# A two-layer GRU with a mixture of experts between its steps: in six groups of steps the experts' products stand behind layer 1's products of a slot instead of behind layer 0's

## The reference

```python
mixed = tanh(x @ W_in.T + b_in + context)
# a GRU layer, twice: h1 = gru(mixed), h2 = gru(h1)
xg = x @ Wih.T + bih                       # for all steps
def step(h, xt):                           # 1024 steps, one after the other
    hg = h @ Whh.T + bhh
    r = sigmoid(xr + hr); z = sigmoid(xz + hz)
    n = tanh(xn + r * hn)
    return (1 - z) * n + z * h
x = x + ((1 + sigmoid(context @ W_gate.T + b_gate)) * h2) @ W_out.T + b_out
# mixture, for every token: a shared expert (512 wide) and 2 of 8 experts (256 wide)
shared = silu(x @ w1) * (x @ w3) @ w2
routed = sum over the 8 experts of combine[e] * (gelu(x @ W1e[e]) @ W2e[e])
out = x + (shared + routed) / 3
```

## Time and profile before

| | |
|---|---|
| median of 3 runs | 2165.33 us (2162.0 to 2167.3) |
| the profiled execution | 2161.73 us, of which the span is 2159.9 us |
| PE, DVE, ACT, POOL busy | 95%, 84%, 52%, 26% of the span |
| granted TensorE clock, mean | 0.996 |

### The profile page before, as it was taken

The page is one execution under the profiler, slowest core; times in us unless marked ns, Lnnn a source line. Parts: engine busy times, 40 slices in busy tenths (PEclk is TensorE's granted clock), DMA queues, the critical chain, the costliest instruction groups (busy, mean ns, idle before and its releaser), DMA issues.

```text
span 2159.9 us, 162405 instructions
## 1 busy us (share of the span) xinstructions
PE 2053.9 (95%) x70040; PEld 1501.7 (70%) x70040; DVE 1816.7 (84%) x11343; ACT 1128.4 (52%) x6471; POOL 563.5 (26%) x2542
## 2 busy tenths in 40 slices
PE   6999999999999999999999999999999999999987
PEld 4666667777677776777767776777767776777766
DVE  3888888888888888988888888888888888888874
ACT  2555555555555555555555555555555555555542
POOL 1222232222322223222232222222232222222220
PEclk9999999999999999999999999999999999999998
DMA  5000000000000000000000000000000000000000
GB/s 221 5 5 5 5 5 5 4 5 5 10 5 5 5 5 10 5 5 5 10 5 5 5 5 10 5 5 5 5 10 5 5 5 10 5 5 9 5 5 9
DMA packets 7184, 24.32 MB, mean 11 GB/s; under 512 B 1584, under 2 KB 3904, under 8 KB 6208
## 3 DMA queue, kind: packets, MB, share of 16 engines
q1 hardware_dynamic: 6464, 13.93, 1.7%
HBM read 11.83 MB, written 2.10 MB: 6 GB/s over the span
## 4 chain that ended last, share of the span: by engine, by line
PE 71%; DVE 19%; ACT 7%; issue 3%; DMA 0%; SPq 0%; POOL 0%; POOLq 0%; DVEq 0%
PE bank L336 34%; PE bank L328 20%; PE bank L268 14%; DVE bank L407 6%; DVE cells L427 5%; ACT factors L477 5%; DVE z_pre L408 3%; PE bank L309 3%; DVE r_pre L398 3%; ACT cells L481 2%; DVE bank L416 0%; PE bank L275 0%; DMA x_t<-in_x_t 0%; DVE x L683 0%; DVE n_second L383 0%
## 5 line engine op out<-in xcount | busy, mean ns | idle before, releaser
L336 PE MATMUL bank<-w_h,cells 128*22 128x128 f32 (+4 forms) x32768 | 1377.8, 281 | 21.2 <-DVE cells L427 11.7
L336 PEld LDWEIGHTS bank<-w_h,cells 128*22 128x22 f32 (+4 forms) x32768 | 865.4, 111 | 127.4 <-DVE cells L427 81.2
L328 PEld LDWEIGHTS bank<-w_h,cells 128*2 128x2 f32 (+15 forms) x28112 | 524.2, 113 | 482.5 <-DVE cells L427 454.5
L522 POOL TENSOR_SCALAR cells<-cells 128x4 f32<-128x4 f32 x2048 | 466.7, 228 | 1497.2 <-DVE cells L427 1496.4
L328 PE MATMUL bank<-w_h,cells 128*2 128x64 f32 (+15 forms) x28112 | 779.4, 225 | 67.8 <-DVE cells L427 55.2
L471 ACT ACTIVATE n_second<-r_pre 128x4 f32<-128x4 f32 x2048 | 426.4, 208 | 517.1 <-DVE r_pre L398 474.4
L477 ACT ACTIVATE factors<-z_pre 128x4 f32<-128x4 f32 x2048 | 429.4, 210 | 473.9 <-DVE z_pre L408 427.0
L427 DVE TENSOR_TENSOR_SCAN cells<-factors,cells 128x18 f32<-128x18 f32 x2048 | 396.5, 194 | 215.5 <-ACT cells L481 140.3
L407 DVE STREAM_TRANSPOSE bank<-bank 128x64 f32<-128x64 f32 x2048 | 522.2, 255 | 56.5 <-PE bank L336 35.0
L398 DVE STREAM_TRANSPOSE r_pre<-bank 128x64 f32<-128x64 f32 x2048 | 483.1, 236 | 34.0 <-PE bank L328 23.5
L408 DVE STREAM_TRANSPOSE z_pre<-bank 128x64 f32<-128x64 f32 x2048 | 428.1, 209 | 0.0
(11 more groups left out here) (90 smaller groups left out, 604.3 us busy)
## 6 DMA issues: line engine op xcount, KB each, us to landing
x_t<-in_x_t SPq DMA_DIRECT2D x4, 512.0 KB, 6.6
w_1e<-in_w_1e SPq DMA_DIRECT2D x1, 2048.0 KB
w_2e<-in_w_2e SPq DMA_DIRECT2D x1, 2048.0 KB
w_x<-in_w_x SPq DMA_DIRECT2D x2, 768.0 KB, 8.1
w_h<-in_w_h SPq DMA_DIRECT2D x2, 768.0 KB, 9.9
w<-in_w SPq DMA_DIRECT2D x3, 512.0 KB
out_y<-y SPq DMA_DIRECT2D x6, 256.0 KB, 3.2
w_in<-in_w_in SPq DMA_DIRECT2D x1, 256.0 KB, 2.3
```

Source lines behind the costliest of these rows:

```text
L328: mm = pe.matmul(r_sums[l][p][32 * g:32 * g + B * (j + 1)], state_tile(l, j, kt), w_h[l][:, kt, g, 2 * U:], start=False, stop=False, tile_ ...
L336: mm = pe.matmul(sums[l][p][32 * g:32 * g + B * (j + 1), 0:width], state_tile(l, j, kt), w_h[l][:, kt, g, 0:width], start=False, stop=Fals ...
L522: pool.tensor_scalar(cell_part(step_rows(l, j), 3), cell_part(step_rows(l, j), 1), 0.5, None, ALU.mult)\
```

## The change

In `Mixture.busy`, for PE in a sparse window, part 0 is now always taken, and part 1 is free except at places 4 and 12. So a product that stood at part 0 (behind layer 0's products, ahead of layer 1's) stands at part 1 (behind layer 1's, ahead of layer 0's of the next slot). Places 0 and 1 become free for products, places 4 and 12 are taken away: 14 of 16 places as before. The rule for windows under 128 slots is as it was. The rules for ACT and DVE are not changed; their operations move only as far as the operands that they wait for do.

```diff
         if engine == "pe":
-            return j in projection_pieces(part ^ 1) or part == 1 and (self.sparse or self.window > 5 * CH and j % 8 != 6)
+            if self.sparse:
+                return part == 0 or j in projection_pieces(0)
+            return j in projection_pieces(part ^ 1) or part == 1 and self.window > 5 * CH and j % 8 != 6
```

## The result

The changed kernel takes 2197.14 us (median of 4 runs, 2195.34 to 2204.66) against 2165.64 before, 31.5 us more. The ratio on record is 1.0162, 95% interval 1.0142 to 1.0182; the two medians by themselves give 1.0145. 2201 was forecast. The change reaches the products of five groups, those with the sparse windows (slots 152 to 791), and not of six as the title has it: the window of the sixth group has 112 slots.

What follows compares the result with a forecast made beforehand. A loop through the engines, with PE serving both layers by turns, was taken as the bound. Moved products +54 us and idle pieces -18 gave +36 on 2161.7, 2198, plus 3.6 for the runs' median: 2201 us, range 2179 to 2226.

Steps and rivals of the forecast that it cites:

- The place of the product: On PE, products at part 1 delay layer 0's next products; a run of seven places costs 0.80 us.
- The first run of places: Places 5 to 11 of a chunk, consecutive products at part 1, slots long and short by turns: 0.80 us.
- Its size: Price of moving 470 sparse-window products to part 1: 0.12 us each, 56 us, less 2 for part 0: +54 us.
- The idle pieces: PE outrunning its instruction supply in sparse windows, 37 us; longer slots remove half: -18 us.
- Rival B: Idle pieces don't depend on the slot's length, so none go: 2219 us, chance 0.17.
- C: All idle pieces go while the products' price stays: 2182 us, chance 0.13.
- Places 0 and 1: Projection on PE delays layer 1's products, some 0.04 us for each of two slots: 0.88 us for that run.
- D: Faster: layer 1's loop shifts forward and absorbs layer 0's delay; up to 2128 us, chance 0.11.
- E: No change: the price is just 0.08 us per product and the pieces go: 2165 us, chance 0.06.
- F: Runs of places are broken, so most products cost the full 0.21 us: 2234 us, chance 0.03.

Runs made afterwards that it cites:

- The run with half of the columns: Sparse-window products stream 128 columns instead of 256: on the changed kernel 2172.5 us (ratio 1.0047), on the kernel before 2161.26 us (0.9993).
- the run with r ahead: DVE takes layer 1's r ahead of layer 0's state scan in sparse windows: 2190.58 us on the changed kernel, ratio 1.0039 on the kernel before.
- the run with odd places: Kernel before with products at part 1 of odd places and part 0 of places 2, 6, 8, 10 and 14: 2198.3 us (ratio 1.0165).

## Why the prediction was right

**The place of the product.** Forecast: layer 0's products 0.48 us behind the state after a plain slot, the slot 0.21 us longer, the next 0.07. The timeline has 0.48, 2.13 (0.22 over 1.91) and 1.96 (0.05). Layer 1's start, forecast at 1.35 us, is at 682.25 - 680.91 = 1.34, and in none of the 640 slots is it sooner than 1.295 us behind layer 0's state. The first run of places costs 0.79 us per chunk by the median slots (forecast 0.80), the second 0.76 (0.88). The run with half of the columns shows that it is PE's time that does it, the run with r ahead that DVE's order keeps layer 1 from making room, and the run with odd places that the price is a matter of the slots' sequence: 0.2 us alone, about half in a run.

**Its size.** +54 us was forecast. It can't be read off by itself, since the pieces fall at the same time, but there are three estimates. The measured +31.5 plus the 11.7 us by which the visible idle pieces fell gives 43. The stretches' +33.7 plus the 15.4 by which the supply's own pieces fell gives 49. The median slots of the table add 1.55 us per chunk, 0.11 for each of 14 products and 52 us for 470. So 0.09 to 0.11 us per product and not 0.12: the term was right or a little large.

**The idle pieces.** They were forecast to halve. The 37 us that the prediction took for them before the change were 34 us over the median slots of the table, of which 25.3 show as pieces. The visible ones went from 25.3 to 13.6 us, those of the supply from 25.2 to 9.8. The three prices above leave 12, 15 and 18 us for this term, against 18 forecast. What is over in one term is over in the other, so the sum (33.7 us in the profile, 36 forecast) does not depend on how the two are parted. The size was a choice halfway between two ends, and that it fits is in part luck. The reason holds: the pieces stand at one point of the blocks of 256, more instructions alone took them to 112 us, less PE time left them or raised them. What the forecast took for their measure, the length of a block in a slot, does not give their sum, as the runs with half of the columns show. Rival B (none go) and C (all go) shared the price of the place and are both ruled out by the 13.6.

**Places 0 and 1.** The 0.04 us that the projection adds to each of two slots is small beside what the run shows: with these two alone at part 1 the two slots behind them cost 2.21 and 2.09 us and the kernel 11 us. In the whole change the median slots of places 1 and 2 are only 0.13 us longer each than before, since they stand in a run.

**The rivals.** D needed layer 1's loop to shift by itself; in the timeline it starts at 1.34 us, not sooner than before. It does shift once DVE takes r earlier, and then only 6.6 us are won. E and F follow from the same reading: the price did not fall to 0.08, and the runs were not broken so far that most products cost the full 0.21.

No version here beats the kernel before.

## What to carry to other kernels

Where two recurrences share an engine by turns, look for each gap's far end: a filler that fits the gap is free ahead of the step whose input is late anyway, and costs its overhang ahead of the step that could have started. Work out the run and not the single slot, since a late slot lends slack to the next; half of a change can cost as much as all of it. And look at the number of instructions as well as at busy time: a slower schedule can win back stalls of the instruction supply, so that two prices don't add.

## What the runs showed of the hardware

PE's instruction supply is a limit of its own here, and it shows at one point of the blocks of 256 instructions, as an idle piece of up to 1.1 us that ends 1.15 to 1.7 us after a packet of the instruction queue has landed. With 144 instructions (matmuls and weight loads) in a slot of 1.92 us there were 25.3 us of idle pieces in the sparse windows; with 160, in the same columns, 112 us on one chip and 87 on another; with 144 in slots of 1.96 and 2.13 us by turns, 13.6; with 128 in 1.91, none. The Trainium skill, "Runtime: NRT & Kernel Launch", section "Instruction fetch mechanics", calls the crossing of a block of 256 mostly hidden; these runs show it hidden in slots with 67 instructions per us and not always in slots with 75.

A change of the stationary tile's width from 32 columns to 128 and back was not free: 0.20 us of idle ahead of the wide weights, 440 times, and in the slot shown 0.20 us more from the product's first matmul to the next step's (0.63 instead of 0.43 us).
